# Layer 0's attention heads: mask addition, negation and row minimum in one VectorE operation that writes the scores to SBUF

## What is computed

```python
content = jnp.einsum('bihd,bjhd->bhij', q + u_bias, k)
pos = jnp.einsum('bihd,jhd->bhij', q + v_bias, p)
pos = _relative_shift(pos)
attn = jax.nn.softmax((content + pos) * scale, axis=-1)
head = jnp.einsum('bhij,bjhd->bihd', attn, v).reshape(B, S, Dm)
return head @ Wo + bo
```

## Time and profile before

| | |
|---|---|
| runs of the kernel before | 2795.24, 2795.57, 2796.34 us |
| median | 2795.57 us |
| the profiled execution | 2793.43 us |
| its span in the profile | 2791.6 us |
| PE busy | 2261.5 us, 81% |
| DVE busy | 1938.2 us, 69% |
| ACT busy | 1553.9 us, 56% |
| POOL busy | 754.9 us, 27% |

### The profile page before, as it was taken

The page is one execution under the profiler, slowest core; times in us unless marked ns, Lnnn a source line. Parts: engine busy times, 40 slices in busy tenths (PEclk is TensorE's granted clock), DMA queues, the critical chain, the costliest instruction groups (busy, mean ns, idle before and its releaser), DMA issues. The chain is left out here.

```text
span 2791.6 us, 53758 instructions
## 1 busy us (share of the span) xinstructions
PE 2261.5 (81%) x17425; PEld 1313.4 (47%) x17594; DVE 1938.2 (69%) x3111; ACT 1553.9 (56%) x2627; POOL 754.9 (27%) x593
## 2 busy tenths in 40 slices
PE   3663999999999999999748777778786488996566
PEld 2231777777777777777513333333332244442222
DVE  3895777777777777777547776677666688885663
ACT  2330666666666666666537668666765255554344
POOL 2555444444444444444101221222123000000000
PEclk9775999999999999999969989989898799998788
DMA  4443111111111111111021112201211222221220
GB/s 158 140 131 108 32 37 35 35 35 35 35 35 35 35 35 35 35 36 33 13 76 44 40 57 83 79 30 57 83 61 48 64 86 83 79 85 64 63 68 23
DMA packets 94932, 163.67 MB, mean 59 GB/s; under 512 B 18120, under 2 KB 44242, under 8 KB 93586
## 3 DMA queue, kind: packets, MB, share of 16 engines
q1 hardware_dynamic: 94866, 162.82, 18.6%
HBM read 102.37 MB, written 60.41 MB: 58 GB/s over the span
## 5 line engine op out<-in xcount | busy, mean ns | idle before, releaser
L1113 ACT ACTIVATE prob<-pair,neg_max_h 128x640 f32<-128x640 f32 x512 | 406.4, 794 | 389.9 <-DVE neg_max_h L1013 389.9
L1013 DVE TENSOR_REDUCE neg_max_h<-pair 128x1 f32<-128x640 f32 x512 | 419.2, 819 | 276.8 <-PE pair L937 271.5
L890 PE MATMUL turn<-ident,prob 128*128 128x128 f32 x2048 | 505.2, 278 | 17.4 <-ACT prob_t L1121 5.5
L1121 ACT COPY prob_t<-turn 128x512 f32<-128x512 f32 x512 | 297.2, 580 | 95.6 <-PE turn L890 93.9
L890 PEld LDWEIGHTS turn<-ident,prob 128*128 128x128 f32 x2048 | 287.5, 141 | 123.4 <-issue 93.5
L1073 POOL TENSOR_TENSOR a_full<-rot_c,rot_s 128x512 f32<-128x512 f32 x128 | 162.2, 1267 | 611.8 <-DVE rot_s L1003 611.8
L1380 DVE TENSOR_TENSOR hid_lo<-hid,hid_hi 128x512 bf16<-128x512 f32 x320 | 279.9, 924 | 67.4 <-ACT hid_hi L1533 66.1
L1911 ACT ACTIVATE prob_h<-pair 128x256 f32<-128x256 f32 (+3 forms) x512 | 205.4, 436 | 195.7 <-PE pair L1798 188.9
L1531 ACT ACTIVATE hid<-pair,up_b 128x512 f32<-128x512 f32 x320 | 228.6, 714 | 56.7 <-PE pair L1585 56.4
L1850 DVE TENSOR_REDUCE row_max<-pair 128x1 f32<-128x128 f32 (+3 forms) x512 | 221.0, 483 | 55.7 <-PE pair L1777 51.3
L1020 DVE TENSOR_TENSOR prob<-prob 128x128 f32<-128x128 f32 x512 | 255.7, 499 | 0.7 <-ACT prob L1113 0.7
(11 more groups left out here) (271 smaller groups left out, 5116.9 us busy)
## 6 DMA issues: line engine op xcount, KB each, us to landing
vx_d<-vx SPq DMA_DIRECT2D x16, 1024.0 KB, 4.7
o_d<-out_sb SPq DMA_DIRECT2D x64, 256.0 KB, 2.1
w_all<-w_d SPq DMA_DIRECT2D x8, 2048.0 KB, 7.0
val<-vx_d SPq DMA_DIRECT2D x32, 256.0 KB, 6.6
val_h<-vx_d SPq DMA_DIRECT2D x32, 256.0 KB
qs_d<-part_q SPq DMA_DIRECT2D x48, 128.0 KB
ks_d<-part_k SPq DMA_DIRECT2D x48, 128.0 KB
num<-o_d SPq DMA_DIRECT2D x24, 256.0 KB
```

The costliest lines, as they stand in the source:

```text
L890: return nc.tensor.transpose(turn_bank[:, jb * P:(jb + 1) * P], prob[s % 4][:, c0:c0 + P], ident[:, :])
L1013: nc.vector.tensor_reduce(neg_max[par][:, s:s + 1], pair[:, S - (ib + 1) * P:2 * S - ib * P], AX_X, ALU.max, negate=True).then_inc(max_don ...
L1113: nc.scalar.activation(prob[s % 4][:, :], pair[:, S - (ib + 1) * P:2 * S - ib * P], ACT.Exp, bias=neg_max[par][:, s:s + 1]).then_inc(exp_d ...
L1121: nc.scalar.copy(prob_t[ib % 2][:, h].rearrange("p b n -> p (b n)"), turn_bank[:, :]).then_inc(kept.sem, 1)
```

## The change

DVE's reduction becomes one operation with an accumulator, `tensor_tensor_reduce`: it adds the mask to the scores, multiplies by -1, writes the 640 results to `prob` in SBUF and takes their minimum into the column of `neg_max`. exp then reads `prob` instead of PSUM, in place, with a scale of -1. The two mask matmuls of each unit go; the unit's last score product now carries `score_ready`. `pair_free` waits for the maximum instead of exp. The wait for the turns of the unit that used the same `prob` buffer moves from ACT to DVE. Ahead of the new operation stands an increment of a semaphore that nobody waits for. Setup builds `pair_mask`, 1024 columns in f32.

```diff
+        pair_mask = sb("pair_mask", [P, 2 * S])
...
+            vec_e.memset(pair_mask[:, :], 0.0).then_inc(setup_dve, 1)
+            v.wait_ge(setup_dve, sat(S_DVE, "no_mask"))
+            vec_e.tensor_copy(pair_mask[:, S - P:S + P], masks_f[:, 2 * P:4 * P]).then_inc(setup_dve, 1)
+            vec_e.tensor_copy(pair_mask[:, S + P:S + P + 1], masks_f[:, 4 * P + 1:4 * P + 2]).then_inc(setup_dve, 1)
...
+            scores_seen = sem(tag + "scores_seen")
...
                 if kind == "score":
-                    pe.wait_ge(exp_done.sem, exp_done.at(UNITS0 * group + n + 1))
+                    pe.wait_ge(max_done.sem, max_done.at(UNITS0 * group + n + 1))
...
-                nc.tensor.matmul(lo_ap, lo_low, pe_hi[:, S:S + low], start=False, stop=False, skip_group_check=True)
-                nc.tensor.matmul(up_ap, lo_up, pe_hi[:, i0:S], start=False, stop=False, skip_group_check=True)
-                nc.tensor.matmul(pair[:, S - P:S], identb[:, :], mask_low, start=False, stop=True, skip_group_check=True)
-                n_up = P + 1 if ib < NB - 1 else P
-                nc.tensor.matmul(pair[:, S:S + n_up], identb[:, :], mask_up[:, 0:n_up], start=False, stop=True,
-                                 skip_group_check=True).then_inc(score_ready.sem, 1)
+                nc.tensor.matmul(lo_ap, lo_low, pe_hi[:, S:S + low], start=False, stop=True, skip_group_check=True)
+                nc.tensor.matmul(up_ap, lo_up, pe_hi[:, i0:S], start=False, stop=True, skip_group_check=True
+                                 ).then_inc(score_ready.sem, 1)
...
-                nc.vector.tensor_reduce(neg_max[par][:, s:s + 1], pair[:, S - (ib + 1) * P:2 * S - ib * P], AX_X,
-                                        ALU.max, negate=True).then_inc(max_done.sem, 1)
+                v.wait_ge(turned.sem, turned.at(UNITS0 * g + s - 3))
+                v.sem_inc(scores_seen, 1)
+                cols = slice(S - (ib + 1) * P, 2 * S - ib * P)
+                nc.vector.tensor_tensor_reduce(prob[s % 4][:, :], pair[:, cols], pair_mask[:, cols], -1.0, 3.0e38,
+                                               ALU.add, ALU.min, neg_max[par][:, s:s + 1]).then_inc(max_done.sem, 1)
...
-                ib = s // GH
-                pair = pairs[place["score", s] % 3]
                 act.wait_ge(max_done.sem, max_done.at(UNITS0 * g + s + 1))
-                act.wait_ge(turned.sem, turned.at(UNITS0 * g + s - 3))
-                nc.scalar.activation(prob[s % 4][:, :], pair[:, S - (ib + 1) * P:2 * S - ib * P], ACT.Exp,
-                                     bias=neg_max[par][:, s:s + 1]).then_inc(exp_done.sem, 1)
+                nc.scalar.activation(prob[s % 4][:, :], prob[s % 4][:, :], ACT.Exp, bias=neg_max[par][:, s:s + 1],
+                                     scale=-1.0).then_inc(exp_done.sem, 1)
```

More of the change, by code:

```diff
@@ L162, in build @@
         setup_store = sem("setup_store")
-        S_DVE = ["eps", "ones", "bias_u", "bias_v", "bias_sh", "identb", "masks", "corner", "pe_hi", "pe_lo", "silu_1p", "silu_r", "silu",
+        S_DVE = ["eps", "ones", "bias_u", "bias_v", "bias_sh", "identb", "masks", "corner", "no_mask", "pair_diag", "pair_corner", "pe_hi", "pe_lo", "silu_1p", "silu_r", "silu",
                  "mods", "plus_ca", "plus_cb", "sign", "abs", "mag", "gate", "lam_p1", "lam_p2", "lam_s1", "lam_s2",
```

## The result

| | before | after |
|---|---|---|
| median of the runs, us | 2795.43 (2789.77 to 2799.20) | 2801.55 (2796.80 to 2808.14) |
| profiled execution, span us | 2793.43, 2791.6 | 2804.81, 2803.0 |
| ratio of times, 95% interval | 1 | **1.0024 (1.0017 to 1.0031)** |

What follows compares the result with a forecast made beforehand. PE looked busy, but turns waited on two chains, through the copy and through exp. Per group -1.76 + 0.44 + 1.48 - 0.26 = -0.10 us; 32 groups -3.2, with setup -1.9: 2794 us, own range 2784 to 2804, wide range 2768 to 2824.

Steps and rivals of the forecast that it cites:

- the turn loop: Last turn of a unit, copy, next unit's first turn, 1.11 us; takes back 4 × 0.11 = +0.44 us per group.
- the exp chain: Scores, maximum, exp, copy, turn two units later, 2.53 us; sets 5 waits per group, adding 5 × 0.295 = +1.48 us.
- (b): Wait for scores on a semaphore instruction ahead of the fused operation: 0.085 us per wait, bounds 0 and 0.17.
- The added wait on turned costs nothing: Ahead of VectorE's fused operation: it asks for turns PE issued a whole unit before the scores are ready; cost 0.
- (a): VectorE's fused operation taken at the reduction's 0.82 us, plus its minimum's read ahead of exp: +0.07, bounds 0 and +0.15.
- (c): ScalarE's exp reads SBUF instead of PSUM: +0.03 us per wait, bounds 0 and 0.06.
- the pair free earlier: Pair of banks free after the maximum instead of exp, removing PE's wait for exp: -0.26 us per group at most.
- the third rival: Fused operation on VectorE slow, at half rate 0.67 us more: at least +2.3 per group, 2870 us or more; chance 0.07.
- the second rival: Between last score product and exp, read held (0.15) and wait 0.17: +0.72 us per group, 2820 us; chance 0.27.
- x: Read plus wait plus exp per wait, forecast 0.185 us; sum zero at 0.20, slower by 0.2% above 0.23.
- the first rival: PE keeps its gain, or a diagonal addition slips ahead of GpSimd's a_lo: 2769 us or about 2771; chance 0.32.
- The sign for the turns: PE's wait for the turns would rise from 85.9 to about 143 us; wrong if below 110 or above 170.

Runs made afterwards that it cites:

- masks left out: Kernel before with the two mask products of each unit left out, nothing fused, scores unmasked: 2773.07 us, ratio 0.9908.
- wait alone: Kernel before with one semaphore instruction ahead of each reduction, carrying the wait for the scores: 2808.84 us, ratio 1.0043.
- one wait: Changed kernel without the fused operation's waits for the turns and the maxima's transpose, which the wait for the scores implies: 2792.11 us, ratio 0.9988.
- exp from the bank: Changed kernel with the mask products kept, exp reading the PSUM bank and the pair released after exp as before: 2822.78 us, ratio 1.0101.
- pair held: Changed kernel with the pair of banks held until exp is done, as before: 2799.84 us, ratio 1.0018.

## Why the prediction was wrong

The time lies inside the forecast's own range of 2784 to 2804; what is wrong is the direction, 0.24% slower where 1.9 us faster was forecast. Step by step, us per group:

| step of the prediction | forecast | measured | by |
|---|---|---|---|
| masks out, less what the turn loop and the exp chain take back of their 0.11 | -0.77 | -0.757 | masks left out |
| (b) the wait on a semaphore instruction | +0.425 | +0.345 | wait alone |
| (b) "The added wait on turned costs nothing", the register instruction set against ACT's | 0 | +0.307, at most 0.045 of it nm_turned | one wait |
| (a) the read, with the fused operation itself | +0.35 | 0.396 - 0.307 = +0.089 | exp from the bank, less wait alone, less the line above |
| (c) exp from SBUF | +0.15 | +0.132 with the release | exp from the bank |
| the pair free earlier | -0.26 | 0 | pair held |
| sum | -0.10 | +0.116 (the change: +0.104) | |

The middle rows are differences of runs, some with the masks and some without, taken so that the fused side comes to its measured 0.873; only masks out, wait alone, one wait and pair held are each a run by itself.

**Two steps failed.** The first is the sentence that the added wait on turned costs nothing. Its reason, that the turns are done a whole unit earlier, is true by the order of PE's program, and it was the wrong question: a wait that is satisfied still takes time on VectorE's sequencer, 0.03 as the second one on an instruction and 0.09 where it needs an instruction of its own (0.66 against 0.57 in slot 0), and behind the wait for the scores this lies on the path. The register instruction of slots 0 to 3 was seen, but set against the one that ACT's exp loses. They don't cancel: in those slots it pushes the wait for the scores onto an instruction of its own, 0.09 in slot 0 and 0.07 behind the copy of the maxima, where VectorE comes last. Taking those waits out brings the change from 0.24% over the kernel before to 0.12% under it. In the swing of 0.2 per group between forecast and result, this term is more than the whole, with nm_turned's part taken off too.

The second is the pair of banks: the row of 7.7 us was taken as a gain "all of it at most", against the rule that the prediction itself used for the masks, that what PE gains ahead of a wait is waited longer there. The run with the pair held puts it at 0.007: the wait came back at one place and went at another, and no time with it.

The read went the other way: the nearest rows, one-column operations, gave +0.07, the bound of nothing was the right one to 0.02, because it runs in the fused operation's tail. The Trainium skill's "VectorE: DVE Perf Modes", section "Two Vector instructions with no wait between them", has it so (by its model a read whose output starts in the same quadrant of partitions as the last output isn't held), and the trace agrees: it starts 0.07 before the fused operation ends. The wait on the semaphore instruction came near by two errors that cancel: it costs 0.11 instead of 0.085, and three places pay it instead of five.

**Two things held.** The masks' side is right to 0.02, and exp's 0.83 too. No stretch of the fused operation beside GpSimd: it runs at 821 ns on the mean of 478, the reduction at 819, so the third rival is out (its 0.67 is 0.66 by its own sum). The halved rate that the Trainium skill's "Vector Engine (DVE) Microarchitecture Reference", section "Points that are easy to get wrong", gives for two sources in SBUF that aren't bf16 does not bear on this operation by its words, one source being in PSUM, and the 821 ns agree.

**Rivals and signs.** The time came from the second rival's side of the edge and for its kind of reason, the way from the scores to exp, though by waits that it didn't name: with x about 0.18 (0.26 to 0.44 in the kernels that keep the masks) + 0.02 + 0.035 = 0.235, just past its 0.23. That this number fits is luck in part, as the five places and the pair's -0.26, with which the edge was worked out, did not hold. Of the first rival, the addition of slot 4 that slips ahead of GpSimd came in one group, and at the price that the prediction gave it, 0.74 against 0.73. In the regular groups it was asked for 0.04 or 0.15 after a_lo's start instead of 0.29, and was held 1.26 or 1.15. The sign that the additions would keep their mean failed, 530 ns against 507; first before, then after:

```profile
L1020 DVE TENSOR_TENSOR prob<-prob 128x128 f32<-128x128 f32 x479 | 242.7, 507 | 0.0
L1026 DVE TENSOR_TENSOR prob<-prob 128x128 f32<-128x128 f32 x478 | 253.3, 530 | 0.0
```

But behind a_lo their length is no measure of the loss, as they end 0.14 to 0.15 after it in any case: the kernel without masks has 544 and is faster, the one with the wait alone 491 and is slower. That end, which I take to be set by the copy of the maxima and the rotations behind it, explains why the masks won nothing up to unit 6: its maximum starts 9.06 after the copy of the maxima in the kernel without masks, 9.07 in the kernel before. The sign for the turns, 143 us with "wrong" below 110, gave 114.1, and 153.6 with the new wait for the addition (39.5).

## What to carry to other kernels

Price an added wait by the instructions that stand between the releasing event and the operation, not by whether its semaphore is late: one more sequencer instruction there cost 0.34 us per group of 16 units here, twice, with a wait and without. Drop waits that another wait implies because one engine signals both in the order of its program, and look at the compiled stream for register instructions that take over a wait. Time that an engine gains ahead of a wait it will make anyway is not a gain, for a released buffer no less than for a removed product; and an operation that is held by another engine should have behind it in its queue only what can wait.

## What the runs showed that I had not expected

- A semaphore instruction without any wait costs as much as one with the wait for the scores, +0.341 against +0.345 us per group, though partly in other places.
- A second wait on the same instruction, long satisfied, costs 0.03 (0.44 against 0.41 from the last product); a separate instruction for it 0.07 to 0.09.
- The read of the accumulator takes 82 ns (mean of 478) and ends with its operation; exp starts as long after the fused operation's start as after the plain reduction's, to 0.02.
- An addition with both operands in SBUF ended 0.14 to 0.15 after GpSimd's operation, whether asked for 0.04 or 0.65 after that one's start.
